# Later own chunks of the neighbour sum without a seed: products with the difference of two one-hots

## The reference, cut to what matters

```python
h = jnp.maximum(_layernorm(x, axis=-1), 0.0)
mask = (adj > 0.0)
xj_proj = h @ W1a
diff = h[:, :, None, :] - h[:, None, :, :]
hh = relu(xj_proj[:, :, None, :] + diff @ W1b + b1)     # (B, N, N, H)
hm = einsum('bjkh,bjk->bjh', hh, mask)
x = x + hm @ W2 + deg[..., None] * b2
```

## Time and profile before

| what | us |
|---|---|
| median of 3 runs | 1949.1 |
| lowest and highest run | 1948.92, 1950.03 |
| span of the profiled execution, first to last instruction | 1947.1 |
| TensorE matmuls busy in the span | 1728.4 |
| VectorE busy in the span | 1313.8 |
| ScalarE and GpSimd busy in the span | 974.0 and 712.6 |
| busy in 1440 to 1947 us (layers 1 to 3): TensorE, VectorE | 434.5, 244.3 |

### The profile page before, as it was taken

One profiled execution on the slowest core, in us unless ns is written; L12 is line 12 of the kernel. 1 busy time (PEld: TensorE's weight loads), 2 busy tenths in 40 slices (PEclk: granted clock), 3 DMA queues, 4 the chain that ended last, 5 costly groups with the idle time before them and its releaser, 6 DMA issues. The chain is left out here.

```text
span 1947.1 us, 49676 instructions
## 1 busy us (share of the span) xinstructions
PE 1728.4 (89%) x13837; PEld 1332.5 (68%) x13838; DVE 1313.8 (67%) x3568; ACT 974.0 (50%) x2265; POOL 712.6 (37%) x866
## 2 busy tenths in 40 slices
PE   1899999999989999999999999999979998995399
PEld 0677676766767676676767676677769887970276
DVE  5687787767878776777878777688834444456633
ACT  2455444545544454554444455454245554744555
POOL 0444444544444454444545444454400000026400
PEclk9999999999999999999999999999989998997699
DMA  5000000000000000000000000000000000000012
GB/s 117 7 12 7 6 6 6 6 6 11 6 6 6 6 6 6 11 6 6 6 6 6 6 6 12 6 0 1 2 0 0 0 0 0 0 0 1 6 40 41
DMA packets 40222, 18.57 MB, mean 10 GB/s; under 512 B 18792, under 2 KB 40106, under 8 KB 40106
## 3 DMA queue, kind: packets, MB, share of 16 engines
q1 hardware_dynamic: 39574, 17.28, 3.7%
q10 hardware_dynamic: 532, 0.21, 0.1%
HBM read 13.29 MB, written 4.19 MB: 9 GB/s over the span
## 5 line engine op out<-in xcount | busy, mean ns | idle before, releaser
L532 PE MATMUL bank<-ac_hi,work 128*128 128x192 f16 x2495 | 535.6, 248 | 0.0
L532 PE MATMUL bank<-ac_lo,work 128*128 128x192 f16 x2495 | 535.5, 248 | 0.0
L722 DVE SCALAR_TENSOR_TENSOR acc<-bank,acc 128x384 f32<-128x384 f32 (+1 forms) x1060 | 467.9, 494 | 25.9 <-PE bank L532 20.0
L789 POOL TENSOR_TENSOR acc<-acc 128x384 f32<-128x384 f32 x256 | 267.5, 1065 | 593.4 <-DVE acc L734 593.4
L524 PE MATMUL bank<-ac_hi,ident 128*128 128x384 f16 (+1 forms) x1060 | 331.2, 312 | 81.2 <-DVE acc L722 58.6
L698 DVE TENSOR_SCALAR work<-work,slot_key 128x896 f16 (+2 forms) x393 | 264.8, 674 | 108.3 <-issue 105.6
L524 PE MATMUL bank<-ac_lo,ident 128*128 128x384 f16 (+1 forms) x1060 | 329.3, 311 | 0.0
L532 PEld LDWEIGHTS bank<-ac_lo,work 128*128 x2495 | 246.7, 99 | 70.7 <-issue 3.7
L532 PEld LDWEIGHTS bank<-ac_hi,work 128*128 x2495 | 246.4, 99 | 71.0 <-issue 3.7
L637 ACT ACTIVATE hmTa<-bank,unscale 128x128 f32<-128x128 f32 x128 | 47.1, 368 | 491.2 <-PE bank L496 491.2
L524 PEld LDWEIGHTS bank<-ac_hi,ident 128*128 128x128 f16 x1060 | 104.5, 99 | 153.6 <-DVE acc L722 85.5
(11 more groups left out here) (204 smaller groups left out, 3330.5 us busy)
## 6 DMA issues: line engine op xcount, KB each, us to landing
adj_in<-in_adj_dram SPq DMA_DIRECT2D x32, 256.0 KB, 2.9
out_dram<-acc SPq DMA_DIRECT2D x32, 128.0 KB, 2.0
l1w<-in_L_gnn_W_dram SPq DMA_DIRECT2D x2, 64.0 KB
l1b<-in_L_gnn_b_dram SPq DMA_DIRECT2D x2, 64.0 KB
x_all<-in_x_dram SPq DMA_DIRECT2D x4, 0.2 KB, 11.8
nm_in<-in_nodemask_dram ACTq DMA_DIRECT2D x1, 64.0 KB
w1a<-in_L_gnn_W_dram ACTq DMA_DIRECT2D x1, 48.0 KB
w1b<-in_L_gnn_W_dram ACTq DMA_DIRECT2D x1, 48.0 KB
```

The costliest lines, as they stand in the source:

```text
L532: last = nc.tensor.matmul(ps[:, t * H:(t + 1) * H], hot, part[:, q, H:2 * H], start=False, stop=(e == 1 and t == slots - 1))
L722: nc.vector.scalar_tensor_tensor(out=sums, in0=bank[n_bank][:, 0:slots * H], scalar=0.0, in1=sums, op0=ALU.min, op1=ALU.add).then_inc(s_fr ...
L789: last = nc.gpsimd.tensor_tensor(t[:, 0:2 * H], t[:, 0:2 * H], t[:, 2 * H:4 * H], ALU.add)
```

## The change

The first own chunk of a graph is done as before. Every later own chunk gets no seed: its banks still hold A + G_old C of the chunk before, and TensorE adds (G_new - G_old) C to them, where G are the one-hots. So `pe_next_chunk` has only the products, with weights from a new buffer `diff` (a ring of two places), and it waits for a new semaphore `s_D` besides `s_free`. VectorE makes the difference, one subtraction of 128x896 f16, right after its read of the first bank of the older chunk (`difference`, passed to `own_chunk` as `after_first`). On TensorE the first chunk is taken out of the loop over own chunks. VectorE computes one more ring place per loop pass.

```diff
+        diff = place(2 * CH)
...
+        s_D = sem("onehot_difference_made")
...
+        def pe_next_chunk(pe, q, regs):
+            cnt, prev, full_prev, pos, diffs = regs
+            pe.reg_mov(prev, cnt)
+            pe.reg_add(cnt, cnt, 1)
+            pe.reg_add(diffs, diffs, 1)
+            at = ring_place(pe, pos, prev, 2)
+            for k, n_bank, first, slots in OWN:
+                ps = bank[n_bank]
+                pe.wait_ge(s_free[k], full_prev if k == 2 else prev)
+                if k == 0:
+                    pe.wait_ge(s_D, diffs)
+                for t in range(slots):
+                    hot = diff[:, ds(at + (first + t) * N, N)]
+                    for part in (ac_hi, ac_lo):
+                        last = nc.tensor.matmul(ps[:, t * H:(t + 1) * H], hot, part[:, q, H:2 * H],
+                                                start=False, stop=True, skip_group_check=True)
+                last.then_inc(s_done[k], 1)
...
         def pe_slots(pe, b, g, u, q, regs, between):
...
-            with pe.Fori(0, n - 1):
-                pe_chunk(pe, q, OWN, ident16[:, :], regs)
+            pe_chunk(pe, q, OWN, ident16[:, :], regs)
+            pe.reg_add(regs[2], regs[2], 1)
+            with pe.Fori(0, n - 2):
+                pe_next_chunk(pe, q, regs)
                 pe.reg_add(regs[2], regs[2], 1)
...
+            def difference(old, new):
+                dve.reg_add(made, cnt, 1)
+                dve.wait_ge(s_G, made)
+                at = ring_place(dve, diff_pos, cnt, 2)
+                nc.vector.tensor_tensor(diff[:, ds(at, CH)], onehot[:, ds(new, CH)], onehot[:, ds(old, CH)],
+                                        ALU.subtract).then_inc(s_D, 1)
+
-            def own_chunk():
+            def own_chunk(after_first=None):
...
                     nc.vector.scalar_tensor_tensor(out=sums, in0=bank[n_bank][:, 0:slots * H], scalar=0.0, in1=sums,
                                                    op0=ALU.min, op1=ALU.add).then_inc(s_free[k], 1)
+                    if k == 0 and after_first is not None:
+                        after_first()
...
             with dve.Fori(0, n - 2) as c:
-                dve_onehot(rs[:, u, q, :, :], SC, c + 1, count())
-                own_chunk()
+                old = ring_place(dve, old_pos, cnt)
+                new = count()
+                dve_onehot(rs[:, u, q, :, :], SC, c + 1, new)
+                own_chunk(lambda: difference(old, new))
```

More of the change, by code:

```diff
@@ L506, in pe_update, with ring_place @@
             nc.tensor.matmul(pU, hmTb[:, p, q * N:(q + 1) * N], w2b[:, :], start=False, stop=True).then_inc(s_W2, 1)
-        def ring_place(eng, pos, chunk):
-            eng.reg_alu(pos, chunk, RING - 1, ALU.bitwise_and)
+        def ring_place(eng, pos, chunk, ring=RING):
+            eng.reg_alu(pos, chunk, ring - 1, ALU.bitwise_and)
             eng.reg_mul(pos, pos, CH)
-            return eng.snap(pos, min_val=0, max_val=(RING - 1) * CH)
+            return eng.snap(pos, min_val=0, max_val=(ring - 1) * CH)
         def pe_chunk(pe, q, banks, node, regs):
-            cnt, prev, full_prev, pos = regs
+            cnt, prev, full_prev, pos, _ = regs
             pe.reg_mov(prev, cnt)
@@ L701, in dve_slots @@
         def dve_slots(dve, b, g, u, q, regs, between):
-            cnt, prev, full, full_prev, pos, count_reg = regs
+            cnt, prev, full, full_prev, pos, count_reg, made, old_pos, diff_pos = regs
             n = dve.snap(count_reg, min_val=MINC + 1, max_val=MAXC)
@@ L804, in _ @@
             def _(pe):
-                regs = [pe.alloc_register(f"pe_{r}") for r in ("chunk", "chunk_before", "own_before", "ring_place")]
+                regs = [pe.alloc_register(f"pe_{r}")
+                        for r in ("chunk", "chunk_before", "own_before", "ring_place", "differences")]
                 pe.reg_mov(regs[0], 0)
                 pe.reg_mov(regs[2], 0)
+                pe.reg_mov(regs[4], 0)
                 pe_adj(pe, 0, 0, 0)
@@ L889, in _ @@
                 regs = [dve.alloc_register(f"dve_{r}")
-                        for r in ("chunk", "chunk_before", "own", "own_before", "ring_place", "slot_chunks")]
+                        for r in ("chunk", "chunk_before", "own", "own_before", "ring_place", "slot_chunks", "onehots")]
+                regs += [dve.alloc_register(f"dve_{r}") for r in ("ring_place_before", "difference_place")]
                 dve.reg_mov(regs[0], 0)
```

## The result

The changed kernel takes **2030.3 us**, the median of four runs (2029.2 to 2036.6), beside 1949.0 (1948.5 to 1950.0) for the kernel before on the same chip: a ratio of 1.0424 [1.0409, 1.0439], **81 us slower**. The forecast was 2004, its range 1950 to 2062. The profiled execution is the slowest of the four, with a span of 2034.8 us against 1947.1: 87.7 more. Budgets of where time went are made on spans, so they come out some 6 us above the medians.

What follows compares the result with a forecast made beforehand. VectorE was taken to bound q = 1 and 2, TensorE q = 0. 31 groups x (0.94 + 0.94 + 0.60 - 0.87) = 50, plus 5 for further chunks, gave 1949.1 + 55 = 2004 us, range 1950 to 2062.

Steps and rivals of the forecast that it cites:

- At q = 1 and 2 VectorE is the bound and TensorE follows it, busy or not: At q = 1 and 2 VectorE sets the pace, although TensorE is busy 92% of a stretch and VectorE 75%.
- the price of the subtraction: On VectorE, each 128x896 f16 subtraction takes 0.62 us, and 1.0 or more while GpSimd's L789 runs.
- rival B: The subtraction on VectorE moves one column a cycle and takes 1.08 us: 57 us more, 2061; chance 0.12.
- A: At q = 1 and 2 VectorE's second one-hot wins the race against GpSimd's L767: 43 us less, 1961; chance 0.19.
- C: The subtraction neither waits for GpSimd nor holds it, mattering at q = 1 and 2: 1921 us; chance 0.13.
- the cancelled case: Subtraction free of GpSimd, but second one-hot still behind L767 at q = 1 and 2: about 1950; chance 0.05.
- GpSimd in turn is held up 0.45: At q = 1 the subtraction delays GpSimd by 0.45 us, so L793 ends at 707.7 instead of 707.28.
- +0.94: Each graph at q = 1 and 2 gets 0.94 us longer: VectorE 1.38 late, less 0.42 or 0.46 of idle time.
- -0.94 a graph in the middle: At q = 0 TensorE is the later engine, so its first transpose comes 0.94 us earlier, at 782.5 instead of 783.43.
- The 9 further own chunks at +0.6 ... are 5: Own chunks beyond two per graph each cost the subtraction's own length, 0.6 us, together 5 us.
- Rival D: TensorE idles longer and falls to half clock at every q = 3: 36 us more, 2040; chance 0.03.
- the loop's end: At nearly every second q = 0, TensorE saves about 0.8 us, as GpSimd is idle at the subtraction there.

Runs made afterwards that it cites:

- VectorE's part alone: Changed kernel with the subtraction made, but TensorE seeding every chunk as before and never waiting for the difference: 1995.9 us.
- TensorE's part alone: Changed kernel without the subtraction; later chunks multiply the plain one-hot without a seed, so their banks hold two chunks' products: 1874.3 us.
- three idle waits: Kernel before plus three VectorE waits per graph, behind the loop over own chunks, on signals given long ago: 1907.6 us.
- spare products: Changed kernel plus 12 TensorE products of 192 columns that nobody reads, ahead of its wait for the difference: 1983.7 us.
- short adds: Kernel before with GpSimd's two adds of 128x384 per graph cut to 16 columns: 1909.2 us.
- three chunks: Kernel before with three chunks in every graph, leaving out the further own chunks: 1932.8 us.

## Why the prediction was right, and where it was not

**Right in what bounds the kernel.** "At q = 1 and 2 VectorE is the bound and TensorE follows it, busy or not" held against a TensorE busy 92% of the time. VectorE's part alone gives the same graphs with all seeds in place, and TensorE's part alone gives 0.3 us a graph there, of 1.15 removed.

**Right in the price of the subtraction.** Forecast 0.62 alone and 1.0 or more beside L789; measured 0.62 and 0.93. The 0.53 that the prediction also worked out did not come. (Its "one L789, 0.95" misreads, where two take 2.11; nothing rests on it.) One column a cycle (rival B) would have been 1.08 alone, so B is out. The later one-hot did run beside GpSimd, as forecast, at 0.86. The Trainium skill (SBUF — State Buffer, "Who interferes with whom") says that a VectorE instruction with two inputs in SBUF contends with a GpSimd one that reads SBUF; these f16 rows agree, 0.93 beside GpSimd against 0.62 alone. Rivals A, C and the cancelled case would have given 1961, 1921 and 1950, and none happened.

**Mis-sized: the hold on GpSimd.** The step "GpSimd in turn is held up 0.45" measured 0.26 (L826 at 0.85 instead of 0.59). With it L801 starts earlier, and the second one-hot, forecast at 1.05 including its wait, takes 0.86. So +0.94 became 0.75 at q = 1 in the even group and 0.83 at q = 2, and +0.60 at q = 3 became 0.45. In the odd group, where the graph that I walked stands, it is 0.48. VectorE's work behind L662 was not "unchanged" there. Before, it stood for 0.31 us in the middle of its small work:

```profile
711.28 0.17 DVE L673 TENSOR_SCALAR left_i<-left 128x4 int32<-128x4 f32 x1 [0.31 <-DVE left L671]
```

That stand is gone in the changed kernel, and in the one with three idle waits q = 1 in the odd group is 0.27 shorter as well, so it belongs to the code's place and not to the subtraction. Over the three places I had 77 us; the budget has 54, with the six slow graphs at q = 3 counted as the others.

**Mis-sized: q = 0.** Forecast -0.94 a graph in the middle, measured -0.58. One such graph, which begins at 731.81: VectorE's last three reads of the first chunk, then TensorE's last product and the transpose.

```profile
734.49 1.27 DVE L752 SCALAR_TENSOR_TENSOR acc<-bank,acc 128x384 f32<-128x384 f32 x3
```

```profile
736.06 0.25 PE L553 MATMUL bank<-ac_lo,work 128*128 128x192 f16 x1
736.37 0.48 PE L495 MATMUL bank<-ident,hm 128*128 128x128 f32 x2
```

The reads end at 735.76, 3.95 us in; the walk had 4.0. But the transpose comes at 4.56 where I had 4.29. I let it follow the last read by 0.3, as if the last bank's products were all but free; they wait for that read, and the step takes 0.6. That is 0.27 of the missing 0.36. Over all q = 0 I had 27 us of gain and the budget has 22.5, with the six followers counted as the others.

**Failed: "The 9 further own chunks at +0.6 ... are 5".** It took the subtraction's length for its cost, as if everything else were ready. In a further chunk nothing is: TensorE waits for one-hot, read and subtraction in a row, 2.13 us, and then loses its clock. 3.2 us each, 29 in all; the runs without them say 27. With the spare products 12.5 are left, so more than half of it is the clock.

**Failed: the clock.** Rival D had the mechanism, a chance of 0.03, and a price that assumed all graphs at q = 3 or none. It came in 6 of them (27 us with their followers) and in the further chunks; with spare products 47 us came back. In part for the same reason the sign "TensorE's busy time down by some 150 us" failed, with 54. I had given the added idle time ahead of the second chunk, 0.9 us, little weight because the only row of half clock stood behind 3.0 us of idle time. Here it came behind 1.36 to 1.40 us and then 0.55. The Trainium skill (TensorE: Matmul & The Clock Gate, "HAM oscillation") describes this as a cost paid anew at each repetition; the traces agree in part: 6 graphs at q = 3 paid it, 22 did not.

**Right for the wrong reason: the loop's end.** Forecast -0.8 each for saved seeds; measured -1.09 in the mean. The three idle waits alone give -3.05. Against that kernel the change *costs* 1.96 a loop end.

**The sum.** Against +55, the budget's 87.5 is 23 less at q = 1 to 3, 4 more at q = 0, 24 more from further chunks and 27 more from the clock at q = 3. 55 - 23 + 4 + 24 + 27 is 87. That the result lay inside the range is partly luck: these errors have both signs, and the gain that comes with the code's length, 41 us in the kernel with three idle waits, is in no term of the sum and hid a part of the price.

## What to carry to other kernels

Before removing work from the busiest engine, follow one unit of work at each place of the loop and see who is waited for: here three places of four gave 0.3 us or nothing for 1.15 us less of TensorE's work, and the same change kept to the fourth, away from the loop's end, was the best kernel. A new wait for an engine costs its own length where other work covers it, but it also costs clock where it doesn't: look at the rare shapes, too, in which nothing is ready ahead. And change an engine's code by a few idle instructions as a control before crediting a gain at a loop's end to the algorithm.

## What the runs showed of the hardware beyond that

**Behind the loop's branch VectorE stands for 2.8 to 4.2 us, and which it is hangs on the code's place.** From VectorE's branch to its next instruction the kernel before takes 3.92 to 4.20 us in each of 13 passes, and so, within 0.15, do the two kernels made from it whose VectorE code has the same length (short adds, three chunks). All the others take 2.8 to 3.1, with a few up to 3.7. TensorE's branch takes 0.16. The trace's instruction queue tells the two apart. Kernel before, 733.40 (the branch) to 737.30; kernel with three idle waits, 714.68 to 717.50 (packets, MB, share of the 16 engines):

```profile
q14 instruction: 2, 0.02, 1.3%
```

```profile
q14 instruction: 1, 0.01, 1.1%
```

Before, one packet of 8 KB starts 0.6 us behind the branch and a second one 1.8 to 2.1 us behind it, and work goes on some 2 us after the second. In all 13 passes of the kernel with the waits the first comes 3.7 to 4.2 us *ahead* of the branch, and one packet 1.0 us behind it is enough. In the changed kernel no packet starts in the 5 us ahead of the branch, and the first behind it comes at 1.0 to 1.3 us. So it looks as if, before, the branch met a fetch of the code behind the loop, and the fetch of its target had to wait for that one. That reading rests on the order of the packets; I moved the code at one place only. The Trainium skill (Runtime: NRT & Kernel Launch, "Instruction fetch mechanics") states that a taken branch out of the fetched window has to wait for a fetch of its target; VectorE's passes agree as far as the packets tell, and no run here shows why TensorE's don't wait.

**Half a clock behind idle times of one to three microseconds, but not behind each of them.** Two graphs at q = 3 of the changed kernel with the same two idle times of TensorE: the first kept full clock, the second fell to half.

```profile
276.97 0.25 PE L553 MATMUL bank<-ac_hi,work 128*128 128x192 f16 x1 [1.36 <-DVE work L737]
...
279.02 0.48 PE L495 MATMUL bank<-ident,hm 128*128 128x128 f32 x2 [0.55 <-POOL hm L827]
```

```profile
810.16 0.26 PE L553 MATMUL bank<-ac_hi,work 128*128 128x192 f16 x1 [1.36 <-DVE work L737]
...
812.21 0.59 PE L495 MATMUL bank<-ident,hm 128*128 128x128 f32 x2 [0.55 <-POOL hm L827]
```

Of the six that fell, four had 1.36 ahead of the second chunk and two 1.39 or 1.40; of the 22 that kept full clock, most had 1.36 and three had 1.39, 1.42 and 1.55. The loop ends say the same: before the change all 13 have an idle time of 3.02 or 3.03 us, and 10 fell; in the changed kernel 2.11 us was followed by half clock in the pass at 600.8 and by full clock in the one at 688.1. Behind the 1.1 to 1.8 us at the loop ends of the kernel with the waits none fell. So the length of the idle time just ahead does not tell which will fall, and what does stays open.

**What the subtraction and GpSimd cost each other.** It lost 0.31 us to GpSimd (0.93 against 0.62) and cost GpSimd 0.26 (0.85 against 0.59), less than its own length.
